# A slot map made by TensorE and gathers per expert, in place of token scatters, in a routed feed-forward kernel

## The reference

```python
w = weights[conditions]                           # one 32x32 matrix per batch
xt = einsum('bct,bcd->bdt', x, w).reshape(T, 256) # T = 1024 tokens
probs = softmax(xt @ gate_w)                      # E = 8 experts
top_p, top_i = top_k(probs, 2); cap = 160
for k in range(2):
    e, w = top_i[:, k], top_p[:, k]
    pos = cumsum(one_hot(e), axis=0)[token, e] - 1
    keep = pos < cap
    buf = zeros((E, cap, D)).at[e, where(keep, pos, cap)].set(xt * keep, mode='drop')
    h = gelu(buf @ w1 + b1)                       # 256 -> 1024
    y = h @ w2 + b2 + gelu(buf @ wd) @ wu         # low-rank branch, rank 32
    out += y[e, min(pos, cap - 1)] * keep * w
sh = gelu(xt @ sw1 + sb1) @ sw2 + sb2 + gelu(xt @ swd) @ swu
return x + out + 0.2 * sh
```

## Time and profile before

| what | value |
|---|---|
| runs | 206.13 us median of 3 (205.58 to 206.89) |
| profiled execution | 205.69 us, its span 203.9 us |
| busy | PE 190.9 us (94%), DVE 134.6 (66%), ACT 132.3 (65%), POOL 111.9 (55%) |
| chain that ended last | POOL 29%, PE 28%, issue 19%, DVE 14%, DMA 5% |
| DMA | 33.04 MB, mean 162 GB/s |

### The profile page before, as it was taken

One profiled execution on the slowest core, in us unless ns is written; L12 is line 12 of the kernel. 1 busy time (PEld: TensorE's weight loads), 2 busy tenths in 40 slices (PEclk: granted clock), 3 DMA queues, 4 the chain that ended last, 5 costly groups with the idle time before them and its releaser, 6 DMA issues.

```text
span 203.9 us, 4113 instructions
## 1 busy us (share of the span) xinstructions
PE 190.9 (94%) x1473; PEld 183.2 (90%) x1473; DVE 134.6 (66%) x295; ACT 132.3 (65%) x282; POOL 111.9 (55%) x162
## 2 busy tenths in 40 slices
PE   6999999999996799999999999999999999999930
PEld 6997778997886799999999999999999999999920
DVE  4588597726941126868969969968968968967020
ACT  2357899706870129959949959859769779678000
POOL 5303204287871025004877867867957958948662
PEclk9999999999999999999999999999999999999995
DMA  5599995122222993057776787687697697501423
GB/s 173 161 304 328 226 299 180 40 101 83 104 96 74 298 335 106 3 206 219 133 243 199 133 257 201 117 261 220 96 279 214 82 290 214 68 0 9 60 32 39
DMA packets 27898, 33.04 MB, mean 162 GB/s; under 512 B 4554, under 2 KB 24772, under 8 KB 27876
## 3 DMA queue, kind: packets, MB, share of 16 engines
q1 hardware_dynamic: 23748, 27.31, 44.1%
q0 software_dynamic: 3760, 4.89, 14.8%
q10 hardware_dynamic: 368, 0.56, 0.8%
HBM read 23.96 MB, written 8.79 MB: 161 GB/s over the span
## 4 chain that ended last, share of the span: by engine, by line
POOL 29%; PE 28%; issue 19%; DVE 14%; DMA 5%; POOLq 1%; ACT 1%; SPq 0%; DVEq 0%
POOL out_rows L402 13%; POOL slot_w L381 6%; POOL slot_rows L424 5%; PE y_ps L815 5%; DVE w_l L600 5%; DVE y_row L741 4%; PE hid_ps L807 3%; PE hid_ps L809 3%; PE hid_ps L808 3%; DVE hid_l L624 3%; PE y_ps L809 2%; PE y_ps L808 2%; PE y_ps L807 2%; DMA out_rows<-y_row,slot_tok 2%; DMA slot_rows<-token_row,slot_i 2%
## 5 line engine op out<-in xcount | busy, mean ns | idle before, releaser
L402 POOL DMA_INDIRECT out_rows<-y_row,slot_tok x24 | 46.1, 1919 | 14.0 <-DVE y_row L741 6.6
L624 DVE TENSOR_TENSOR hid_l<-gelu_f,hid_h 128x320 fp32r<-128x320 f32 (+1 forms) x80 | 41.1, 529 | 13.8 <-ACT hid_h L528 12.8
L807 PE MATMUL hid_ps<-xs_h,w_h 128*128 128x288 f32 x128 | 38.2, 298 | 0.0
L809 PE MATMUL hid_ps<-xs_h,w_l 128*128 128x288 f32 x128 | 37.6, 294 | 0.0
L808 PE MATMUL hid_ps<-xs_l,w_h 128*128 128x288 f32 x128 | 37.6, 294 | 0.0
L359 POOL CAST wd_h<-wd_raw 128x64 fp32r<-128x64 f32 x27 | 10.1, 411 | 46.9 <-DMA wd_raw<-in_L_ffn_wd 46.3
L527 ACT ACTIVATE gelu_f<-hid_ps,bias_now 128x320 f32<-128x320 f32 x64 | 35.0, 547 | 1.1 <-PE hid_ps L809 0.4
L528 ACT ACTIVATE hid_h<-hid_ps,bias_now 128x320 fp32r<-128x320 f32 x64 | 35.4, 552 | 0.0
L600 DVE TENSOR_TENSOR w_l<-w_raw,w_h 128x512 fp32r<-128x512 f32 x36 | 26.3, 749 | 12.5 <-POOL w_h L370 11.8
L809 PE MATMUL y_ps<-hid_h,w_l 128*128 128x288 f32 x112 | 32.9, 294 | 0.0
L808 PE MATMUL y_ps<-hid_l,w_h 128*128 128x288 f32 x112 | 32.9, 294 | 0.0
(11 more groups left out here) (182 smaller groups left out, 422.5 us busy)
## 6 DMA issues: line engine op xcount, KB each, us to landing
w_raw<-in_L_ffn_w SPq DMA_DIRECT2D x16, 1024.0 KB
slot_rows<-empty_row SPq DMA_DIRECT2D x1, 2600.0 KB, 16.9
slot_in<-slot_rows SPq DMA_DIRECT2D x8, 260.0 KB, 3.6
x_in<-in_x SPq DMA_DIRECT2D x2, 512.0 KB, 4.3
w_raw<-in_L_ffn_sw SPq DMA_DIRECT2D x1, 1024.0 KB
out_rows<-base SPq DMA_DIRECT2D x2, 512.0 KB, 4.4
wu_raw<-in_L_ffn_wu SPq DMA_DIRECT2D x24, 32.0 KB
slot_in<-slot_rows SPq DMA_DIRECT2D x8, 65.0 KB, 3.7
```

What stands on the lines that cost most here:

```text
L402: pool.indirect_dma_start(out=out, out_offset=bass.IndirectOffsetOnAxis(ap=slot_tok[par][0:n, s:s + 1].bitcast(U32), axis=0), in_=y_row[0: ...
L624: dve.tensor_tensor(hid_l[:, j - 1, 0:n], gelu_f[:, j % 3, 0:n], hid_h[:, j - 1, 0:n].bitcast(F32), ALU.subtract).then_inc(hid_split, 1)
L807: pe.matmul(out_ap, l_h, r_h, start=start, stop=False)
L809: return pe.matmul(out_ap, l_l, r_h, start=False, stop=stop)
```

## The change

POOL no longer scatters tokens. SP writes the token rows once to DRAM (1 MB, `x_rows`), in two halves, and each expert's slots are gathered from there by three indirect DMAs (`gather`), two experts ahead. The map from slots to tokens is made on chip: a slot in an expert is a tile number (0 to 2) and a place in the tile (0 to 127). DVE makes for each token and choice the place (`place_of`) and a one-hot over expert and tile (`keyed`, 24 wide), times three values: token number plus one, weight's high part, weight's low part (`key_values`, 72 wide). POOL makes one-hots of the place (`at_place`, 16 comparisons of 128x128). PE multiplies the two, 16 products summed in one bank (`map_slots`), after tile 1 of the second half. DVE's `side_data` then makes from it, for all experts at once, the rows to gather, the rows to scatter to and the weights. POOL's `side_data` and `set_bias` in the periods, the second copy of the rows, the fill and SP's `load_slots` are gone; ACT reads the biases from `bias_t`. The zero rows of the output are written later.

```diff
             for h in range(2):
+                sp.wait_ge(rows_copied, (h + 1) * NT // 4)
+                half = slice(h * HTILES, (h + 1) * HTILES)
+                sp.dma_start(x_rows_v[:, half, :], token_row[:, half, :]).then_inc(x_rows_out[h], 16)
...
-            sp.wait_ge(dispatched, 16 * NT * K)
-            sp.wait_ge(consts, 11)
-            load_slots(0, 0, first=True)
-            load_slots(1, 1, first=True)
...
+            def gather(e, par):
+                if e >= 2:
+                    pool.wait_ge(slots_turned, (e - 1) * KD)
+                for s in range(ST):
+                    n = ST_ROWS[s]
+                    pool.indirect_dma_start(
+                        out=slot_in[par][0:n, s, :], out_offset=None, in_=x_rows,
+                        in_offset=bass.IndirectOffsetOnAxis(ap=slot_src[0:n, e, s:s + 1].bitcast(U32),
+                                                            axis=0)).then_inc(slots_in[par], 16)
...
+            pool.wait_ge(places_known, 1)
+            for k in range(K):
+                for t in range(NT):
+                    pool.tensor_scalar(at_place[:, t, k, :], place_number[:, :], place_of[:, t, k:k + 1], None,
+                                       ALU.is_equal).then_inc(at_place_made, 1)
+
+            pool.wait_ge(slots_sided, 1)
+            for h in range(2):
+                pool.wait_ge(x_rows_out[h], 16)
+            gather(0, 0)
+            gather(1, 1)
+
+            def period(e, par, split=True):
+                if split and e + 2 < E:
+                    gather(e + 2, par)
                 if split:
-                    small_hi(e + 2, par)
+                    wd_hi_part(e + 2, par)
+                    wu_hi_part(e + 2, par)
...
-                side_data(e, par)
...
             def period(e, par, split=True, turned=True):
-
-                act.wait_ge(bias_set, e + 1)
...
+            def make_values():
                 dve.engine_nop().then_inc(chosen_made, 1)
-                step(dve.tensor_tensor(picked[:, :, :, :], chosen[:, :, :, :], slot_base[:, :, :, :], ALU.mult))
-                step(dve.tensor_reduce(base_of[:, :, :], picked[:, :, :, :], AX_X, ALU.add))
+                step(dve.tensor_copy(values[:, :, :, 1].bitcast(F32R), weight[:, :, :]))
+                step(dve.tensor_tensor(values[:, :, :, 2], weight[:, :, :], values[:, :, :, 1], ALU.subtract))
...
-                step(dve.tensor_tensor(base_of[:, :, 1], base_of[:, :, 1], best[:, :], ALU.add))
...
+                step(dve.tensor_scalar(slot_f[:, :, :], pos[:, :, :], float(CAP), PAST_END, ALU.is_ge, ALU.mult))
+                step(dve.tensor_tensor(pos[:, :, 1], pos[:, :, 1], best[:, :], ALU.add))
+                step(dve.tensor_tensor(slot_of[:, :, :], pos[:, :, :], slot_f[:, :, :], ALU.add))
+                step(dve.tensor_scalar(tile_past[:, :, :], slot_of[:, :, :], float(P), None, ALU.is_ge))
+                step(dve.scalar_tensor_tensor(out=tile_of[:, :, :], in0=slot_of[:, :, :], scalar=float(2 * P),
+                                              in1=tile_past[:, :, :], op0=ALU.is_ge, op1=ALU.add))
+                dve.scalar_tensor_tensor(out=place_of[:, :, :], in0=tile_of[:, :, :], scalar=-float(P),
+                                         in1=slot_of[:, :, :], op0=ALU.mult, op1=ALU.add).then_inc(places_known, 1)
+                step(dve.tensor_tensor(in_tile[:, :, :, :], tile_of[:, :, :].unsqueeze(3).to_broadcast([P, NT, K, ST]),
+                                       tile_number[:, :, :, :], ALU.is_equal))
+                for k in range(K):
+                    ins = dve.tensor_tensor(keyed[:, :, k, :, :], ...)
+                step(ins)
+                for k in range(K):
+                    dve.tensor_tensor(key_values[k], ...).then_inc(keyed_made, 1)
...
+            def side_data():
+                dve.wait_ge(map_made, 1)
...
+            def map_slots():
+                pe.wait_ge(keyed_made, K)
+                for k in range(K):
+                    for t in range(NT):
+                        pe.wait_ge(at_place_made, k * NT + t + 1)
+                        ins = pe.matmul(turn_ps[1][:, 0:VALUES * E * ST], at_place[:, t, k, :],
+                                        key_values[k][:, t, :, :].rearrange("p v g -> p (v g)"),
+                                        start=(k == 0 and t == 0), stop=(k == K - 1 and t == NT - 1))
+                ins.then_inc(map_made, 1)
...
                     hidden(h, j, 0, 0, xct_h, xct_l, cols, HALF)
                     if h == 0 and j == HT - 3:
                         count_before()
+                    if h == 1 and j == 1:
+                        map_slots()
```

More of the change, by code:

```diff
@@ L32 @@
 ROW = D + 4
-W_COL, ID_COL = D, D + 1
+VALUES = 3
 ST = (SLOTS + P - 1) // P
@@ L86, in build @@
         picked = sb("picked", [P, NT, K, E])
-        base_of = sb("base_of", [P, NT, K])
         pos = sb("pos", [P, NT, K])
         slot_f = sb("slot_f", [P, NT, K])
-        slot_i = sb("slot_i", [P, NT, K], I32)
+        slot_of = sb("slot_of", [P, NT, K])
+        tile_past = sb("tile_past", [P, NT, K])
+        tile_of = sb("tile_of", [P, NT, K])
+        place_of = sb("place_of", [P, NT, K])
+        in_tile = sb("in_tile", [P, NT, K, ST])
+        keyed = sb("keyed", [P, NT, K, E, ST])
+        weight = sb("weight", [P, NT, K])
+        values = sb("values", [P, NT, K, VALUES])
+        at_place = sb("at_place", [P, NT, K, P], F32R)
+        slot_w = sb("slot_w", [P, E, ST])
+        slot_free = sb("slot_free", [P, E, ST])
+        slot_row = sb("slot_row", [P, E, ST])
+        slot_tok = sb("slot_tok", [P, E, ST], I32)
+        slot_src = sb("slot_src", [P, E, ST], I32)
         gate_raw = sb("gate_raw", [P, KD, E])
@@ L102, in build @@
         cond_diag = sb("cond_diag", [P, NT, P])
-        token_row = [sb(f"token_row{k}", [P, NT, ROW]) for k in range(K)]
+        token_row = sb("token_row", [P, NT, D])
         base = sb("base", [P, NT, D])
@@ L106, in build @@
         xct_l = sb("xct_l", [P, KD, T], F32R)
[L107 to L112, removed]
+        slot_in = [sb(f"slot_in{i}", [P, ST, D]) for i in range(2)]
         xs_h = sb("xs_h", [P, KD, SLOTS], F32R)
         xs_l = sb("xs_l", [P, KD, SLOTS], F32R)
+        key_values = [x[:, :, :].rearrange("p k n -> p (k n)")[:, 0:NT * VALUES * E * ST].rearrange(
+            "p (t v g) -> p t v g", t=NT, v=VALUES) for x in (xs_h, xs_l)]
         y_t = sb("y_t", [P, KD, SLOTS])
@@ L429, in period @@
[L429 to L438 removed]
+            wd_hi_part(0, 0)
+            wu_hi_part(0, 0)
+            wd_hi_part(1, 1)
@@ L443, in _ @@
-            pool.wait_ge(base_out, 32)
-            pool.wait_ge(spare_out, 16)
-            for e in range(1, E - 1):
+            for e in range(E - 1):
                 period(e, e % 2)
-            period(7, 1, split=False, biases=False)
+            period(7, 1, split=False)
             combine(7, 1)
@@ L711, in place_tokens @@
                 step(dve.tensor_reduce(pos[:, :, :], picked[:, :, :, :], AX_X, ALU.add))
-                dve.tensor_scalar(slot_f[:, :, :], pos[:, :, :], float(CAP), PAST_END, ALU.is_ge,
-                                  ALU.mult).then_inc(slots_known, 1)
-                step(dve.tensor_tensor(base_of[:, :, :], base_of[:, :, :], pos[:, :, :], ALU.add))
-                dve.wait_ge(slots_known, 1)
-                dve.tensor_tensor(slot_i[:, :, :], base_of[:, :, :], slot_f[:, :, :], ALU.add).then_inc(slots_known, 2)
+                step(dve.tensor_scalar(slot_f[:, :, :], pos[:, :, :], float(CAP), PAST_END, ALU.is_ge, ALU.mult))
@@ L772, in _ @@
                     w2_chunk(j - 1, 1, 1)
+                if j == 1:
+                    side_data()
             for t in range(HTILES, NT):
```

151 lines of the change are left out of this document (61 added, 90 removed).

## The result

The kernel before took 208.05 us in the median of 20 runs (205.58 to 210.45), the changed one 205.87 us in the median of 20 (204.67 to 207.16). The ratio is 0.9933, with a 95% interval of 0.9904 to 0.9962: a little faster, by more than the measurement is uncertain, where I had forecast 206.5 us and 0.4 us slower. The time I gave is within 0.7 us. What I compared it with was wrong: the three runs of before that I had gave 206.13 us, and the kernel before has two groups of runs, as the experiments show.

What follows compares the result with a forecast made beforehand. PE's own work, its single stall and the tail were taken to bound the kernel. The terms -2.8 + 1.6 + 0.6 + 1.85 - 0.85 summed to +0.4, giving 206.5 us, range 204.2 to 209.6.

Steps and rivals of the forecast that it cites:

- Step 1: At the transposes of expert 0's slots, PE's single wait for their load goes whole: -2.8 us.
- The gathers' own chain: Expert 0's map, then three gathers on POOL ending at 58.8 us, landed at 62.4, six us to spare.
- Step 2: DVE's longer placement delays its first shared row, so PE stalls at the third shared tile: +2.2 us, crossing included.
- The crossing: POOL's 16 comparisons beside DVE's key products hold DVE up: 0.6 us, between 0 and 1.2.
- The rival in which POOL holds DVE: DVE's products wait for all POOL's comparisons, total 211.4 us; chance 0.22 together with a dearer map.
- Step 3: The map's 16 matmuls of 72 columns on a PE without gaps, 0.115 us each: +1.85 us.
- cover: At the map, POOL's comparisons are done at 49 us, PE asks at 50.9: hidden by 2 us.
- Step 4: Expert periods unchanged: 0 us; POOL goes from 11.4 to about 12.7 us busy in 15, still under PE.
- Step 5: In the tail, combine(6) and all behind it come earlier without POOL's side_data: -0.85 us.
- a rival: The tail gives its bound as combine(6)'s slow first scatter shrinks, map cheap, no crossing: 204.1 us; chance 0.14.
- my bound of 1.86: In the tail, the most that could come, since PE's last tile is ready to scatter by about 197.0, against 198.86.
- the forecast case: The summed steps, 206.5 us, spanning 205.1 to 208.0 with the bounds of steps 2 and 3; chance 0.60.

Runs made afterwards that it cites:

- the run with the waiting POOL: The changed kernel with POOL's 16 comparisons held until DVE's key products are done; 204.98 us in one run.
- the kernel with the tail's edits alone: The kernel before with ACT reading biases from bias_t without waiting for POOL's copy, and w2's high part ahead of side_data; 205.02 us, ratio 0.9813.
- after's second trace: The changed kernel run again with nothing changed; 205.66 us (12 runs), ratio 0.9939 to the kernel before.
- one index: The kernel before with expert 0's slot transposes moved one shared output tile later; 203.39 us, ratio 0.9852.

## Why the prediction was wrong

**Step 1 failed, in its size.** I priced the stall at its length, 2.8 us, and its length did go: the table of stages has -2.99 at that place. What I didn't count is that in 47 of 67 runs the clock fell to half at this wait, and those runs took 2.6 us more. The earlier trace rows come from a run in which it hadn't fallen, and by their times the three runs behind 206.13 us were all of the rarer kind, by luck. So the true step is about -2.8, or -5.4 in the mean of the runs where the clock fell, and against the typical run of before that alone is the change's gain. The gathers' own chain was right to 0.2 us on POOL (58.96 for 58.8); their landing, which I put at 62.4, no view here shows, but PE had no wait for it.

**Step 2, right in place, 0.3 too much.** The wait sits at the third shared tile. Without POOL the way takes 3.68 us (41.1 - 37.42 was my sum, the same). The crossing is 0.2 us, not 0.6. PE's table lists 1.6 us of wait, counted from the modelled end of the last matmul; from start to start PE loses 1.8, and 0.1 more at the first product behind the wait, so the stage is 1.90 us longer for my 2.2. The rule of the Trainium skill (SBUF — State Buffer, Who interferes with whom), taken strictly, would have made it 1.8 by my rows; here DVE's six two-input operations lost 0.2 us in all, and POOL paid. The rival in which POOL holds DVE (211.4 us) is refuted by the same rows.

**Step 3, right by size, with a wrong cover.** 16 matmuls of 72 columns start within 51.45 to 53.15, 0.106 us each for my 0.115, and the stage grew by 1.50 us with the faster 512-column products in it (54 x 0.0055 = 0.30 us), so 1.8 for the map. The comparisons took 0.77 us each and not 0.35: I scaled from a 3-wide one and a 512-wide copy, and with DVE's products out of their way they are still 0.70 apart (11.26 / 16), 0.58 where DVE stands still. They end at 51.92 for my 49, half a us behind the map's first matmul. PE didn't wait only because its last matmul, which starts at about 53.0, is the one that needs the last comparison: about 1 us of cover for my 2, and none where the comparisons start later, as the run with the waiting POOL shows.

**Step 4, right.** The periods add 0.01 us over 118. POOL has 13.3 us in 15 for my 12.7, since each gather is 1.11 us plus the issue, as priced.

**Step 5, right in its term, 0.4 too small at the end.** The combine starts 0.80 us earlier, as worked out (0.85). The first scatter also shrank by 0.9 us, which I had left to a rival, and the last one starts 1.87 us earlier against the last product, which is my bound of 1.86. The end gained 1.23, because the stretch from the last scatter's start to the end took 203.95 - 198.23 = 5.72 us for 5.08. Why, no run here settles; in the kernel with the tail's edits alone it took 5.43, and in after's second trace 6.25, so that there the end gained only 0.6. From the last product to the end it is 7.4 to 8.1 us in five traces of kernels with the changed tail, and 8.5 to 9.0 in the seven with before's.

**Not foreseen at all:** the 512-column products, -0.6 us (0.28 in the first half and 0.30 in the second). The sum has no term for them. It comes from the placement in SBUF, which changed with the buffers that the change removed and added.

**The sum again.** My +0.4, with -0.3 (step 2), -0.4 (tail), -0.6 (512 columns) and -0.2 (stall), gives -1.1, the first two traces' -1.08. With after's second trace it is -0.5, all of the difference in the tail, and the runs at full clock differ by as little, 205.7 to 206.18. So without the clock the change is 0.4 to 1.1 us quicker, where I had it 0.4 slower. The step to the medians' 2.2 us is the clock. In the range, one sum was wrong too: with the upper bounds of both steps (0.6 and 1.55 more) the forecast case ends at 208.6 and not at 208.0.

## What to carry to other kernels

A wait of PE costs its length and perhaps a stretch at half clock with it: compare the granted clock of many runs before pricing it, and don't trust a median of three. Before a stall's cause is rebuilt, try the work it holds up one tile later: here one index gave 2.6 us and rid the kernel of the clock's fall, while the rebuilt map paid 3.7 us on PE (1.9 of stall and 1.8 of products) to save the same. And where a change removes buffers, look at the cadence of unchanged matmuls, since their placement moved too.

## What of the hardware was unexpected

- The same wait can cost its length alone or nearly twice that: in 20 of 67 runs of one kernel the clock stayed full, in 47 it fell. In six traces the waits of 2.7 and 2.8 us go with none or 3.4 us at half clock, those of 3.2 to 3.5 us with 6.8.
- An unchanged stream of fp32r products of 512 columns ran at 0.228, 0.230 or 0.2335 us each by where its operands lie in SBUF, 32 bytes making the difference; those of 256 and 288 columns didn't react.
- POOL needs 0.58 us for a 128x128 comparison with a scalar for each partition where DVE stands still, and 0.70 in the mean with DVE's weight splits beside it (its copies, four times as wide, take 0.62 in the mean).
